# A two-layer graph network on 256 nodes: two classes' softmax weights combined ahead of the edge loop, and the mixed tiles scattered in two fp32r products

## The chip, the cores and the metric

The kernel runs on one core of a Trainium2 chip. The time is that of the device for one execution, in microseconds (us), the median of several runs; lower is better. PE is TensorE, DVE is VectorE, ACT is ScalarE, POOL is GpSimd, and SP is the engine that only starts DMAs here.

## The reference, cut to what matters

There are N = 256 nodes with D = 1024 features and E = 8192 edges sorted by destination. Each edge gets a logit, in one of three classes by its position in the list, the logits are turned into softmax weights per destination, and z is the weighted sum of the source rows. A node update and a layer norm follow, and a second attention layer behind them.

```python
feat = concatenate([n_f[edge_src], n_f[edge_dst]], axis=1)
e_hh = relu(feat[:128] @ W_hh + b_hh)
e_oo = relu(feat[128:768] @ W_oo + b_oo)
e_ho = relu(feat[768:] @ W_ho + b_ho)          # 7424 of the 8192 edges
logit = (concatenate([e_hh, e_oo, e_ho]) @ W_a + b_a)[:, 0]
ex = exp(logit - segment_max(logit)[edge_dst])
alpha = ex / segment_sum(ex)[edge_dst]
z_f = segment_sum(alpha[:, None] * n_f[edge_src], edge_dst)
nf2 = concatenate([n_f, z_f], axis=1)          # then W_hn, W_on, relu, residual, layer norm
```

## The kernel before

Edges are not handled by their weights one at a time. For each class the kernel sums logits and counts into 256 x 256 tables, `S_log` and `S_cnt`, with three kinds (0 is hh, 1 is oo, 2 is ho) and two halves h of 128 destinations each. The mean logit of a (source, destination) pair is sum by count, and the softmax over a destination's row is exp(mean - maximum) times count. P, the normalised sum of the three kinds, is transposed on PE (`PT`) and multiplied with the node features to give z (`zT`).

Weights W come by DMA in chunks of 128 rows, two a transfer, into four slots of `W_raw`, are split into a high fp32r part (`high`, on ACT, L580) and a low part (`low`, W minus high, on DVE at L906, or `lows`, on POOL at L458, for those chunks that `by_pool` names), and PE multiplies high with high, high with low and low with high. A slot is loaded again when its chunks have been used. Chunks 40 to 47 are the last half of W_ho, 48 to 79 are W_hn and W_on (`update`), 80 to 87 layer two's W. UX is 58: chunks 48 to 57 need only the node features, those from 58 on come around zT.

The hh and oo classes are small and are summed ahead of the loop. DVE forms their mean logits (`static_means`, L1078) and their row maximum in `small[:, 44:46]` (L1154 and L1155, stage "means"), while PE ends the chunks of W_ho. DVE then takes the lows of `B_tab` (L1104), for which ACT takes the highs (L657), and ACT copies the same accumulators out for the mixed rows (`target_rows`, L704). The stage "hoB_lo" behind them releases PE's second half of the first gather.

The ho class has 7424 edges, sorted by (source quarter, destination quarter) into 58 tiles of 128 edges with one pair of quarters each (NL = 58), and 4 tiles that hold what is left over from several pairs, the mixed tiles (NM = 4). For each of the 58 tiles the loop does this:

- ACT makes one-hot columns for two tiles at a time (`distance`, `onehot`, double-buffered).
- PE gathers the two table rows of each edge with them, summed in PSUM (`gather`, L1539, four fp32r products of 512 columns). There are three PSUM places, so gather t waits for the reduction of tile t - 3.
- DVE reduces each row with relu and W_a to a logit (`reduce_tile`, L1167).
- POOL makes one-hots of the keys for the scatter (`ends`), and ACT scales one of them by the logit (`scale_ends`, L692).
- PE scatters tile t - 4 into G0, the table in PSUM, logits and counts at once (`scatter`, L1554, fp32).

A mixed tile's rows are fetched by POOL's indirect DMAs, reduced on DVE ahead of the tiles in `AHEAD` (`reduce_mixed`, L1173), scaled on ACT over all four quarters (`mixed_ends`, L712), and scattered on PE `MLAG` tiles later in four fp32 products of 256 columns (`scatter_mixed`, L1548). Its one-hots `mixed_dst` and `mixed_src` are made by POOL ahead of the loop (`mixed_onehots`), in memory that later takes the highs of chunks 56 and 57 and the third kind of `S_log` and `S_cnt`.

Behind the loop PE does two chunks of the update, the last four scatters and the chunks 50 to 56. DVE copies the third kind out, forms its means and the maxima (stage "maxima"), and takes the low of chunk 56. ACT takes the exponentials of all three kinds for each half (L767), DVE multiplies and adds them (L1194 to L1196), normalises (stage "P"), takes the low of chunk 57, and copies PT (L1207). PE waits for P, transposes it, does chunk 57, and goes on to zT (L1626). In each engine the order is that of the program, with semaphores between the engines; `link` makes DVE or POOL wait for its own last instruction.

## Time and profile before

| | us |
|---|---|
| median of 3 runs | 339.38 (338.69 to 339.42) |
| the profiled execution's own time | 340.16 |
| its span, first to last instruction | 338.1 |
| PE busy | 316.6 (94%) |
| DVE busy | 281.7 (83%) |
| ACT busy | 187.4 (55%) |
| POOL busy | 121.6 (36%) |

The profile is of one execution, so durations out of it are held against its own time and not against the median. Busy shares are means over stages with different limits. Starts are in us from the first instruction. A matmul's duration contains its way through the array and overlaps with the next, so the price of one in a row of them is the distance of the starts. The granted clock of PE stands at 1.00 for 2.4 GHz and at 0.50 for 1.2 GHz.

### The profile page before, as it was taken

To read this page: it belongs to the slowest core of one execution; us is meant where nothing else is said; L and a number is where in the kernel's file an instruction comes from. 1 tells how busy PE (TensorE), PEld (TensorE's weight loads), DVE (VectorE), ACT (ScalarE), POOL (GpSimd) and SP (SyncE) were. 2 spreads that over 40 slices of the span, in tenths; PEclk is the share of its full clock that TensorE was granted. 3 is DMA by queue.
4 is the path that set the end of the run, shared out by engine and by line. 5 is a ranking of instruction groups with operands and counts; after the bars stand their busy time and mean duration, and the time that the engine had idled before them with its cause. 6 is when DMAs were issued, how large, how long until landed. Compare 5 with 4: busy or idle time off the path is not lost.

```text
span 338.1 us, 4491 instructions
## 1 busy us (share of the span) xinstructions
PE 316.6 (94%) x1438; PEld 243.4 (72%) x1438; DVE 281.7 (83%) x414; ACT 187.4 (55%) x283; POOL 121.6 (36%) x126
## 2 busy tenths in 40 slices
PE   8999999999999999889899999999799899999980
PEld 8778887776654678567788888887587686788730
DVE  0998999998979988799898998989968967883644
ACT  3765593412036336588776867657048567851355
POOL 4300042075000591819997999770000300005000
PEclk9999999999999999999999999999799999999996
DMA  7999599869999999214606303024397999000003
GB/s 220 402 404 410 193 342 381 322 239 229 281 345 305 392 416 409 106 62 75 175 2 121 123 7 126 1 64 155 101 364 245 297 339 356 8 1 0 2 1 124
DMA packets 19351, 68.86 MB, mean 204 GB/s; under 512 B 2413, under 2 KB 2413, under 8 KB 19329
## 3 DMA queue, kind: packets, MB, share of 16 engines
q1 hardware_dynamic: 13536, 50.07, 40.3%
q0 software_dynamic: 3232, 12.41, 13.4%
q10 hardware_dynamic: 2560, 6.10, 5.1%
q8 instruction: 13, 0.21, 0.3%
q14 instruction: 10, 0.07, 0.1%
HBM read 63.31 MB, written 5.26 MB: 203 GB/s over the span
## 4 chain that ended last, share of the span: by engine, by line
PE 47%; DVE 38%; ACT 5%; DMA 5%; issue 4%; POOL 0%; DVEq 0%; ACTq 0%; POOLq 0%
DVE ps L1167 10%; PE ps L1539 8%; DVE W_lo L906 7%; PE ps L1662 7%; PE ps L1371 6%; PE ps L1420 6%; PE ps L1591 5%; DMA W_raw<-in_L_gnn_W_oo_dram 5%; PE ps L1599 3%; DVE tile_val L925 2%; PE ps L1694 2%; PE ps L1626 2%; PE ps L1548 2%; PE ps L1554 1%; PE ps L1404 1%
## 5 line engine op out<-in xcount | busy, mean ns | idle before, releaser
L580 ACT CAST W_hi<-W_raw 128x1024 fp32r<-128x1024 f32 x62 | 63.0, 1047 | 51.6 <-DMA W_raw<-in_L_gnn_W_ho_dram 28.1
L1167 DVE SCALAR_TENSOR_TENSOR ps<-ps,wa_bc 128x1024 f32<-128x1024 f32 x58 | 69.2, 1253 | 5.6 <-PE ps L1539 5.6
L906 DVE TENSOR_TENSOR W_lo<-W_raw,W_hi 128x1024 fp32r<-128x1024 f32 x54 | 66.1, 1255 | 7.1 <-ACT W_hi L580 4.6
L1371 PE MATMUL ps<-W_hi,xT_hi 128*128 128x512 f32 x112 | 45.8, 409 | 0.8 <-DVE W_lo L906 0.8
L1539 PE MATMUL ps<-A_tab,oh 128*128 x116 | 41.8, 441 | 3.4 <-DVE ps L1167 3.3
L1371 PE MATMUL ps<-W_lo,xT_hi 128*128 128x512 f32 x112 | 43.7, 390 | 0.0
L1539 PE MATMUL ps<-B_tab,oh 128*128 x116 | 36.5, 396 | 0.9 <-DVEq L899 0.9
L1371 PE MATMUL ps<-W_hi,xT_lo 128*128 128x512 f32 x112 | 34.5, 389 | 0.0
L487 POOL TENSOR_SCALAR sc<-sc 128x256 f32<-128x256 f32 x29 | 28.4, 978 | 2.6
L1420 PE MATMUL ps<-W_raw,hh_x 128*128 128x512 f32 x64 | 28.2, 594 | 0.0
L686 ACT ACTIVATE oh<-oh_dist 128x512 fp32r<-128x512 bf16 x29 | 18.2, 628 | 14.6 <-PE ps L1539 14.5
L1539 PEld LDWEIGHTS ps<-B_tab,oh 128*128 128x128 f32 x116 | 21.7, 188 | 6.0 <-issue 1.3
L1371 PEld LDWEIGHTS ps<-W_hi,xT_hi 128*128 128x128 f32 x112 | 21.0, 188 | 6.8 <-issue 1.8
L485 POOL TENSOR_TENSOR sc<-irow,keys 128x256 f32<-128x256 f32 x29 | 20.9, 722 | 11.8 <-PE ps L1554 11.6
L1554 PEld LDWEIGHTS ps<-sc 128*128 128x128 f32 x116 | 21.4, 188 | 4.9
L1371 PEld LDWEIGHTS ps<-W_lo,xT_hi 128*128 128x128 f32 x112 | 21.1, 188 | 4.6 <-issue 0.7
L1371 PEld LDWEIGHTS ps<-W_hi,xT_lo 128*128 128x128 f32 x112 | 21.0, 188 | 4.5
L1539 PEld LDWEIGHTS ps<-A_tab,oh 128*128 128x128 f32 x116 | 18.3, 190 | 6.0 <-issue 5.6
L1420 PEld LDWEIGHTS ps<-W_raw,hh_x 128*128 128x128 f32 x64 | 11.9, 190 | 13.5 <-issue 13.4
L692 ACT ACTIVATE sc<-sc,keys 128x64 f32<-128x64 f32 x58 | 17.9, 339 | 6.2 <-DVE ps L1167 6.2
L679 ACT ACTIVATE oh_dist<-key_rows,pcol 128x512 bf16<-128x512 uint8 x29 | 20.5, 707 | 0.4 <-ACT mixed_row L704 0.4
L558 POOL TENSOR_SCALAR x<-x 128x2048 f32<-128x2048 f32 x1 | 5.5, 5467 | 41.5 <-DVEq L899 41.5
(328 smaller groups left out, 642.3 us busy)
## 6 DMA issues: line engine op xcount, KB each, us to landing
W_raw<-in_L_gnn_W_ho_dram SPq DMA_DIRECT2D x8, 1024.0 KB, 7.3
W_raw<-in_L_gnn_W_hh_dram SPq DMA_DIRECT2D x8, 1024.0 KB, 8.6
W_raw<-in_L_gnn_W_hn_dram SPq DMA_DIRECT2D x8, 1024.0 KB, 5.9
W_raw<-in_L_gnn_W_on_dram SPq DMA_DIRECT2D x8, 1024.0 KB, 6.8
W_raw<-in_L_gnn_W_oo_dram SPq DMA_DIRECT2D x7, 1024.0 KB, 12.1
W_raw<-in_L_gnn_W_dram SPq DMA_DIRECT2D x4, 1024.0 KB, 6.9
table_scratch<-tabs ACTq DMA_DIRECT2D x2, 1024.0 KB, 5.7
key_rows<-key_rows_scratch POOLq DMA_DIRECT2D x1, 1792.0 KB, 13.3
```

The source lines that it names most:

```text
L485: link(ga.tensor_tensor(pair, irow[:, 1:Q + 1].unsqueeze(1).unsqueeze(1).broadcast_to([P, 2, 2, Q]), keys[:, t:t + 2, 0:2].unsqueeze(3).br ...
L487: ga.tensor_scalar(pair, pair, 0.0, None, ALU.is_equal).then_inc(ends_made, 1)
L580: sa.copy(halves(n)[0], W_raw[:, n // 2 % NS, n % 2, :]).then_inc(hi_made, 1)
L679: sa.activation(oh_dist[:, j % 2, :, :], key_rows[:, :, 2 * j * P:2 * (j + 1) * P], ACT.Abs, bias=pcol[:, 1:2]).then_inc(dist_made, 1)
L686: sa.activation(oh[:, j % 2, :, :], oh_dist[:, j % 2, :, :], ACT.Relu, bias=1.0, scale=-1.0) \
L906: v.tensor_tensor(lo, W_raw[:, n // 2 % NS, n % 2, :], hi.bitcast(F32), ALU.subtract).then_inc(lo_made, 1)
L1167: v.scalar_tensor_tensor(acc, acc, 0.0, wa_bc[:], ALU.max, ALU.mult, accum_out=keys[:, t, 2:3]).then_inc(reduced, 1)
L1371: ins = mm(acc[:, m * D + f:m * D + f + 512], x_part(n - first, m), W[:, f:f + 512], start=(n == first and x_part is hi and W is W1), stop ...
L1420: ins = mm(G0[:, f:f + 512], hh_x[:, row // KC, row % KC, :], W_raw[:, n // 2 % NS, n % 2, f:f + 512], start=(row == 0), stop=(row == 2 * ...
L1539: ins = mm(acc[:, n * 512:(n + 1) * 512], oh[:, t // 2 % 2, k, t % 2 * P:(t % 2 + 1) * P], tab[:].rearrange("p q d -> p (q d)")[:, n * 512 ...
L1554: ins = mm(G0[:, bass.ds(column.with_bounds(min_val=0, max_val=15 * Q), Q)], sc[:, t % U, 1:3, :].rearrange("p r n -> p (r n)"), sc[:, t % ...
L1662: ins = mm(G1[:, m * D + f:m * D + f + 512], part[:, c, m * P:(m + 1) * P], W[:, f:f + 512], start=(c == 0 and part is xT_hi and W is W1), ...
```

## The change

It has four parts.

1. hh and oo: the exponentials of the two kinds are taken ahead of the loop, against their own maximum, multiplied by the counts and added there. Behind the loop only the third kind gets its exponential, and the combined part is rescaled by exp(own maximum - common maximum), a column of two values, inside the instruction that adds it.
2. Mixed tiles: the one-hots become fp32r, the logits are split into a high and a low fp32r part, and each mixed tile is scattered in two sets of four fp32r products, the second set (with the counts' one-hots set to zero) MLAG tiles behind the first. ACT gets a step `mixed_rest` between them.
3. AHEAD goes from (18, 24, 36, 42) to (18, 24, 33, 39), MLAG from 6 to 5.
4. The low of chunk 57 (UX - 1) goes from DVE, where it stood between P and PT, to POOL, behind its `pick` and `shift` constants. Chunk 56 stays with DVE.

`static_L`, `behind_L` and their like are second names for the memory of `S_log` and `S_cnt`.

```diff
-AHEAD = (18, 24, 36, 42)
-MLAG = 6
+AHEAD = (18, 24, 33, 39)
+MLAG = 5
...
-            return END["hoB"] <= n < UX - 2
+            return END["hoB"] <= n < UX and n != UX - 2
...
             ga.nop().then_inc(pick_made, 1)
+            lows(UX - 1, UX)
...
-                sa.activation(mixed_dst[:, r, :, 1, :], mixed_dst[:, r, :, 0, :], ACT.Copy, scale=mixed_logit[:, r:r + 1]) \
-                  .then_inc(mixed_made, 1)
+                sa.activation(mixed_dst[:, r, :, 1, :], mixed_dst[:, r, :, 0, :].bitcast(F32), ACT.Copy,
+                              scale=mixed_logit[:, r:r + 1]).then_inc(mixed_made, 1)
+                sa.copy(mixed_hi[:, r:r + 1], mixed_logit[:, r:r + 1]).then_inc(mixed_parts, 1)
+
+            def mixed_rest(r):
+
+                act.wait_ge(mixed_parts, 3 * r + 1)
+                sa.activation(mixed_lo[:, r:r + 1], mixed_hi[:, r:r + 1].bitcast(F32), ACT.Identity,
+                              bias=mixed_logit[:, r:r + 1], scale=-1.0).then_inc(mixed_parts, 1)
+                act.wait_ge(mixed_scattered, 2 * r + 1)
+                act.wait_ge(mixed_parts, 3 * r + 2)
+                sa.activation(mixed_dst[:, r, :, 1, :], mixed_dst[:, r, :, 0, :].bitcast(F32), ACT.Copy,
+                              scale=mixed_lo[:, r:r + 1]).then_inc(mixed_parts, 1)
+                act.wait_ge(mixed_parts, 3 * r + 3)
+                sa.activation(mixed_dst[:, r, :, 0, :], mixed_dst[:, r, :, 0, :].bitcast(F32), ACT.Copy,
+                              scale=0.0).then_inc(mixed_made, 1)
...
             table_high(B_tab, G1, 2, 4, 0, D // 2)
+            act.wait_ge(dve_step, dve_at("means"))
+            for h in range(2):
+                sa.activation(S_log[:, 0:2, h, :], S_log[:, 0:2, h, :], ACT.Exp, bias=small[:, 42 + h:43 + h]) \
+                    .then_inc(act_step, 1)
...
                     if (AHEAD[r] + 4) // 2 == j:
                         mixed_ends(r)
+                    if (AHEAD[r] + MLAG + 4) // 2 == j:
+                        mixed_rest(r)
...
             act.wait_ge(dve_step, dve_at("maxima"))
+            sa.activation(small[:, 42:44], small[:, 8:10], ACT.Exp).then_inc(act_step, 1)
             for h in range(2):
-                sa.activation(S_log[:, :, h, :], S_log[:, :, h, :], ACT.Exp, bias=small[:, h:h + 1]) \
+                sa.activation(S_log[:, 2, h, :], S_log[:, 2, h, :], ACT.Exp, bias=small[:, h:h + 1]) \
                     .then_inc(act_step, 1)
...
+            link(v.tensor_scalar(small[:, 42:44], small[:, 44:46], -1.0, None, ALU.mult))
             stage("means")
             low_quarter(B_tab, G1, 4, 0, 2)
             stage("hoB_lo0")
             low_quarter(B_tab, G1, 6, 2, 4, 0, D // 2)
+            dve.wait_ge(act_step, act_at("static1"))
+            link(v.tensor_tensor(S_log[:, 0:2, :, :].rearrange("p k h n -> p (k h n)"),
+                                 S_log[:, 0:2, :, :].rearrange("p k h n -> p (k h n)"),
+                                 S_cnt[:, 0:2, :, :].rearrange("p k h n -> p (k h n)"), ALU.mult))
             low_quarter(B_tab, G1, 8, 2, 4, D // 2, D // 2)
             stage("hoB_lo")
+            link(v.tensor_tensor(S_log[:, 0, :, :], S_log[:, 0, :, :], S_log[:, 1, :, :], ALU.add))
...
             link(v.tensor_scalar(small[:, 0:2], small[:, 2:4], -1.0, None, ALU.mult))
+            link(v.tensor_tensor(small[:, 8:10], small[:, 44:46], small[:, 2:4], ALU.subtract))
             stage("maxima")
             low(UX - 2)
             for h in range(2):
                 dve.wait_ge(act_step, act_at(f"soft{h}"))
-                link(v.tensor_tensor(S_log[:, :, h, :], S_log[:, :, h, :], S_cnt[:, :, h, :], ALU.mult))
-                link(v.tensor_tensor(S_log[:, 0, h, :], S_log[:, 0, h, :], S_log[:, 1, h, :], ALU.add))
-                link(v.scalar_tensor_tensor(S_log[:, 0, h, :], S_log[:, 0, h, :], 1.0, S_log[:, 2, h, :],
+                link(v.tensor_tensor(S_log[:, 2, h, :], S_log[:, 2, h, :], S_cnt[:, 2, h, :], ALU.mult))
+                link(v.scalar_tensor_tensor(S_log[:, 0, h, :], S_log[:, 0, h, :], small[:, 42 + h:43 + h], S_log[:, 2, h, :],
                                             ALU.mult, ALU.add, accum_out=small[:, 4 + h:5 + h]))
...
             stage("P")
-            low(UX - 1)
...
-                if t - MLAG in AHEAD:
-                    scatter_mixed(AHEAD.index(t - MLAG))
+                for part in range(2):
+                    if t - (1 + part) * MLAG in AHEAD:
+                        scatter_mixed(AHEAD.index(t - (1 + part) * MLAG), part)
```

## Rows read from the trace of the kernel before

**Rows 1.** The page, part 4: the chain that ended last, shares of the span.

```profile
PE 47%; DVE 38%; ACT 5%; DMA 5%; issue 4%; POOL 0%; DVEq 0%; ACTq 0%; POOLq 0%
```

**Rows 2.** The waits, 142 to 222: who waited for whom, us, times, longest.

```profile
DVE ps L1167 <- PE ps L1539: 5.6, 7, 1.6
```

**Rows 3.** Timeline of DVE in the loop: start, us, what, [idle before].

```profile
142.93 1.23 DVE L1167 SCALAR_TENSOR_TENSOR ps<-ps,wa_bc 128x1024 f32<-128x1024 f32 x1 [0.95 <-PE ps L1539]
...
186.10 1.23 DVE L1167 SCALAR_TENSOR_TENSOR ps<-ps,wa_bc 128x1024 f32<-128x1024 f32 x1 [1.57 <-PE ps L1539]
...
211.18 1.23 DVE L1167 SCALAR_TENSOR_TENSOR ps<-ps,wa_bc 128x1024 f32<-128x1024 f32 x1 [1.23 <-PE ps L1539]
...
220.60 1.26 DVE L1167 SCALAR_TENSOR_TENSOR ps<-ps,wa_bc 128x1024 f32<-128x1024 f32 x1
```

**Rows 4.** The chain in order of time, merged: start, us, what, up to the loop's end.

```profile
115.73 1.33 PE ps L1452 x12
...
208.43 1.78 PE ps L1548 x8
...
213.61 0.99 PE ps L1539 x4
214.77 0.98 PE ps L1539 x4
...
222.46 0.85 PE ps L1554 x8
```

**Rows 5.** Windows: us, busy of PE, PEld, DVE, ACT, POOL; clock, DMA share, GB/s.

```profile
200.00:210.00 10.00, 10.00 (x53) 8.57 (x51) 9.95 (x18) 6.79 (x16) 9.24 (x10) 1.00 0.30 107
...
240.00:244.00 4.00, 4.00 (x13) 3.13 (x13) 3.85 (x5) 0.00 (x0) 0.00 (x0) 0.64 0.00 0
```

**Rows 6.** Timeline of all engines ahead of the loop, 126 to 146.

```profile
134.32 0.69 DVE L1154 TENSOR_TENSOR junk<-S_log 128x512 f32<-128x512 f32 x1
...
135.88 4.04 DVE L1104 TENSOR_TENSOR B_tab<-ps,B_tab 64x1024 fp32r<-64x1024 f32 x4
...
138.45 1.01 ACT L704 COPY bias_bc<-ps 128x1024 f32<-128x1024 f32 x1 [1.00 <-DVEq L899]
...
140.56 1.42 DVE L1104 TENSOR_TENSOR B_tab<-ps,B_tab 64x512 fp32r<-64x512 f32 x2 [0.64 <-ACT B_tab L657]
...
142.17 0.72 PE L1539 MATMUL ps<-B_tab,oh 128*128 x2 [0.88 <-DVEq L899]
```

**Rows 7.** The chain in order of time behind the maxima, 230 to 300.

```profile
233.06 0.88 DVE S_log L1194
...
233.97 0.44 DVE S_log L1195
...
236.82 0.18 DVE small L1199
...
238.30 1.24 DVE lo_in_raw L906
...
239.59 2.07 PE ps L1591 x4
241.66 2.03 PE ps L1599 x6
...
268.52 0.91 PE ps L1591 x4
```

**Rows 8.** Timeline of PE, 235 to 262: the transposes of P.

```profile
238.27 0.66 PE L1615 MATMUL ps<-ident,S_log 128*128 128x128 f32 x4 [1.73 <-DVEq L899]
```

**Rows 9.** Groups by line: count, busy us, mean ns of one, idle before.

```profile
L712 ACT ACTIVATE mixed_dst<-mixed_dst,mixed_logit 128x256 f32<-128x256 f32 x4 | 2.0, 496 | 0.0
```

**Rows 10.** Timelines of DVE and POOL: a DVE reduction from SBUF, two POOL lows.

```profile
200.40 1.25 DVE L1173 SCALAR_TENSOR_TENSOR mixed_row<-mixed_row,wa_bc 128x1024 f32<-128x1024 f32 x1
...
200.99 2.93 POOL L458 TENSOR_TENSOR W_lo<-W_raw,W_hi 128x1024 fp32r<-128x1024 f32 x1
...
208.89 2.38 POOL L458 TENSOR_TENSOR lo_in_raw<-W_raw,hi 128x1024 fp32r<-128x1024 f32 x1
```

More of the change, by code:

```diff
@@ L100, in gnn_two_layers @@
         mixed_logit = sb("mixed_logit", [P, NM])
+        mixed_hi = sb("mixed_hi", [P, NM], F32R)
+        mixed_lo = sb("mixed_lo", [P, NM])
         st_logit = sb("st_logit", [P, 1 + JO])
@@ L136, in gnn_two_layers @@
         before_sums.close()
+        before_S = ExitStack()
+        static_L = sb("static_L", [P, 2, 2, N], F32, before_S)
+        behind_L = sb("behind_L", [P, 2, N], F32R, before_S)
+        static_C = sb("static_C", [P, 2, 2, N], F32, before_S)
+        behind_C = sb("behind_C", [P, N], F32R, before_S)
+        before_S.close()
         S_log = sb("S_log", [P, 3, 2, N])
@@ L191, in gnn_two_layers @@
         mixed = ExitStack()
-        mixed_dst = sb("mixed_dst", [P, NM, N // Q, 2, Q], F32, mixed)
+        mixed_dst = sb("mixed_dst", [P, NM, N // Q, 2, Q], F32R, mixed)
         mixed.close()
         hi_01 = sb("hi_01", [P, 2, D], F32R, regions)
-        behind_hi_01 = sb("behind_hi_01", [P, 2 * P], F32, regions)
+        behind_hi_01 = sb("behind_hi_01", [P, 2 * P], F32R, regions)
         key_rows = sb("key_rows", [P, 2, NL * P], U8, regions)
@@ L217, in gnn_two_layers @@
         mixed_rows = [b_ho_bc[:], bias_bc[:, 1, :], bias_bc[:, 0, :], mixed_row[:]]
-        mixed_src = [behind_hi_01[:, 0:N], S_log[:, 2, 0, :], S_log[:, 2, 1, :], S_cnt[:, 2, 0, :]]
+        mixed_src = [behind_hi_01[:, 0:N], behind_L[:, 0, :], behind_L[:, 1, :], behind_C[:]]
         tab_dram = [nc.dram_tensor(f"table{k}_scratch", [N, D], F32, kind="Internal").ap() for k in range(2)]
@@ L259, in gnn_two_layers @@
         mixed_made = sem("mixed_made")
+        mixed_parts = sem("mixed_parts")
         mixed_scattered = sem("mixed_scattered")
@@ L358, in gnn_two_layers @@
                      "x1T0a", "x1T0b", "x1T1", "h_0", "h_1", "albc", "sums", "hp0", "hp1", "hp2"]
-        ACT_STAGES = ["xT0a", "xT0b", "xT1", "hh_x", "ooB_out", "C_hh", "C_oo", "A_rows0", "A_rows1", "L_oo", "L_hh", "B_rows0", "B_rows1", "counts", "parts", "soft0", "soft1", "zT0", "both0", "zT1",
+        ACT_STAGES = ["xT0a", "xT0b", "xT1", "hh_x", "ooB_out", "C_hh", "C_oo", "A_rows0", "A_rows1", "L_oo", "L_hh", "static0", "static1", "B_rows0", "B_rows1", "counts", "parts", "rescale", "soft0", "soft1", "zT0", "both0", "zT1",
                       "both1", "q0_low", "q1_low", "sd0", "x1T0a", "sd1", "x1T0b", "x1T1", "h1_0", "h1_1a",
@@ L737, in _ @@
                     if j // 3 == 8:
-                        act.wait_ge(mixed_scattered, NM)
+                        act.wait_ge(mixed_scattered, 2 * NM)
                     high(END["hoB"] + j // 3)
@@ L1542, in gather, with scatter_mixed @@
                 ins.then_inc(gathered, 1)
-            def scatter_mixed(r):
-                pe.wait_ge(mixed_made, r + 1)
+            def scatter_mixed(r, part):
+                pe.wait_ge(mixed_made, 2 * r + part + 1)
                 for q in range(N // Q):
-                    ins = mm(G0[:, q * N:(q + 1) * N], mixed_dst[:, r, q, :, :].rearrange("p r n -> p (r n)"), mixed_src[r],
-                             start=False, stop=False, skip_group_check=True)
+                    ins = mm(G0[:, q * N:(q + 1) * N], mixed_dst[:, r, q, :, :].rearrange("p r n -> p (r n)"),
+                             mixed_src[r], start=False, stop=False, skip_group_check=True)
                 ins.then_inc(mixed_scattered, 1)
```

## The prediction

> **What bounds the kernel now.** I read the page's chain first: PE holds 47% and DVE 38% of what ended last [rows 1], so no engine bounds the whole kernel, and each edit has to be placed in its own stage. The diff touches three: the softmax statistics ahead of the 58-tile loop, the loop, and the softmax behind it.
>
> In the loop the list of waits says that DVE waited 5.6 us for PE's gathers [rows 2]. DVE back to back takes 1.18 us a tile: the starts 211.18 and 220.60 are eight tiles apart [rows 3]. With four reductions of mixed tiles at about 1.2 us its work is 58 x 1.18 + 4 x 1.2 = 73.2 us, and the loop lasted 79 us (142.93 to 220.60 + 1.26 [rows 3]). PE takes 0.99 us for a gather and 1.16 us with its scatter (the starts 213.61 and 214.77 [rows 4]), plus 1.78 us for the products of each mixed tile [rows 4]: 58 x 1.155 + 4 x 1.78 = 74.1 us (1.155 over many tiles). The two are even, so what costs is a PE burst larger than its lead. Two of the four mixed scatters made DVE idle, 1.57 us before the start at 186.10 and 1.23 before 211.18 [rows 3]; with the 0.14 us by which back-to-back reductions otherwise overlap their accumulator read that is 1.71 and 1.36 us. The rest of the 5.6 us lies in small gaps in the first 15 tiles, ahead of any mixed scatter.
>
> Behind the loop DVE is the chain: means, maxima, softmax, then the low half of the last chunk [rows 7]. PE has finished what it may do and stands idle for 1.73 us before the four transposes of P [rows 8], then 0.66 us more for that low half, and then runs its ten products in 2.07 + 2.03 us [rows 7], at a mean clock of 0.64 between 240 and 244 [rows 5]. Everything behind (zT, the rest of the update, layer two) hangs on the end of these products at 241.66 + 2.03 = 243.69: chunks, DVE lows and DMAs there are released by it or in step with it.
>
> **The change part by part.**
> *Ahead of the loop.* DVE gets one tiny operation (0.2 with its gap, as the row at 236.82 [rows 7]) before "means", and one product over 1024 columns between the B_tab lows. From 0.88 us for 768 columns [rows 7] and 0.69 for 512 [rows 6] I take 1.2 us. DVE finished its four first lows at 139.92 and began the last two at 140.56, after 0.64 us of idle time [rows 6]. Now it is at 140.1 + 1.2 = 141.3: +0.7 us (bounds 0.3, if the idle time takes more of it, and 1.4, if nothing does). ACT's two new exponentials (512 columns each, between 0.5 and 0.93 us by their neighbours; 0.65 taken) follow the B_tab copies that ended by 137.5 and end at 138.75. ACT's next item began at 138.45 [rows 6], so it slips 0.3 us, which DVE's 0.7 covers. The sum of two classes (0.69 us) comes after the last low and lies beside PE's 0.72 us of the first gather's second half [rows 6]: nothing; without that cover 0.7.
>
> *The loop.* Each mixed tile's four fp32 products (eight passes in the trace, 1.78 us, 0.22 each) become two sets of four fp32r products. No fp32r row has 256 columns. The nearest below is bf16 with 256 columns, 12 in 1.33 us, 0.111 each; above stands the full price of the fp32 product, 0.445 [rows 4], and between them fp32r with 512 columns, 0.227 (four in 0.91 us [rows 7]). Since 512 fp32r columns cost twice 0.111 and a little, I take 0.115: 0.46 us a set, eight sets 3.7 us instead of 7.1. PE's sum falls to 70.7 us, under DVE's 73.2, and a burst of 0.46 us fits under the lead that a gather has over its reduction (about a microsecond when PE is held back by its three buffers). Both gaps go, -3.07 us. Sets fall on neighbouring tiles (28 and 29, 43 and 44), where two bursts use up the lead: 0.27 given back. Net -2.8 us (0 to -3.3). The other 2.8 us of DVE's idle time stay.
> ACT pays: per mixed tile two more full activations (0.50 us, as the first [rows 9]), two on one column (0.2 each) and their waits, 1.4 us, 5.6 us in all. It was busy 6.79 of 10 us in 200 to 210 [rows 5]. mixed_rest waits for the first set on PE, and queued behind it on ACT are the next onehots, for which gathers wait. By then DVE has reduced that same tile (scale_ends stands ahead of it), so PE is past the set: no wait. At tiles 38 to 45 a high, two rests and an ends meet and the onehots run some 0.2 to 0.6 us late, under PE's lead. Nothing taken; up to 1.5. POOL writes the same one-hots; DVE's reductions of mixed tiles 2 and 3 move three tiles forward, and their rows have landed before.
>
> *Behind the last reduction.* The last scatters no longer queue behind a late update, but ACT's copy of the counts, which DVE needs next, follows the last scale and a high at an unchanged distance: -0.2 of the 0.5 us possible. Maxima gets a subtraction: +0.2. Then DVE has two rounds of 0.88 + 0.44 for product and sum and about 0.46 for the weighted sum, 3.76 us from 233.06 to 236.82; now 0.44 + 0.45 a round, 1.8 us: -1.96 (0.44 is the 256-column row [rows 7]). ACT's one-column exponential and two of 256 columns (0.3 + 0.5 until the first is ready) lie beside the low of chunk 56, 1.22 us on DVE; without it they would show.
>
> *The last chunk's low.* It leaves DVE, 1.24 us between P and the copy of PT [rows 7], and PE's wait for it, 0.66 us, goes. POOL has it (2.38 us [rows 10]) after its memsets; its earlier lows keep their place, and it should end near 225.5, eight us before use. PE's chunks 50 to 56 end at 236.5 - 2.6 = 233.9 (they follow the last scatter, which comes earlier by the loop's 2.1 and the 0.5); P is ready at 238.2 + 0.7 - 2.8 - 0.2 + 0.2 - 1.96 = 234.1. PE's idle time falls from 1.73 + 0.66 to some 0.3 us. The trace shows the clock at half only after those 2.4 us of standing, so I take it to stay at 2.4 GHz: the ten products cost 10 x 0.227 = 2.27, the price of such products elsewhere [rows 7], not 4.10: -1.83 (0 to -1.83).
>
> **Sum**, against the profiled execution (span 338.1, time 340.16): +0.7 - 2.8 - 0.2 + 0.2 - 1.96 - 0.66 - 1.83 = -6.55, so 333.6. It stands 0.78 over the median 339.38 of the three runs, which gives 332.8. What is late next is DVE through the loop, and behind it PE and DVE within 0.3 us of each other.
>
> **Rivals.**
> *A, slower: the fp32r products cost as much as the fp32 ones.* Then PE has 4 x 1.78 = 7.1 us more, less about 1.1 that it now waits for DVE, plus 0.7: the last gather is 6.7 us later. P is at 238.2 + 6.7 + 0.2 - 1.96 = 243.1, PE just done, zT starts at 243.1 + 0.7 + 2.3 = 246.2, +2.5: 341.9. It decides from about 1.47 us a set (2.5 / 8 under 1.78). Against it: the fp32r rows show one pass for each product, not two, and at 512 columns twice what bf16 costs at 256. 4%.
> *B, a product bound by its weight load, 0.227.* A set is 0.91, eight 7.3 us: DVE's gaps stay in smaller pieces. -6.55 + 2.8 = -3.75: 335.6. Against it: a scatter pass with its load takes 0.106 (eight in 0.85 us [rows 4]). 10%.
> *C, ACT comes late* in tiles 38 to 50, 1.5 us: 334.3. For it: 1.4 us per mixed tile on an engine two thirds busy. 10%.
> *D, PE's clock falls before zT all the same*: 334.7. 8%.
> *E, POOL's low in DVE's way.* At 200.99 a POOL low took 2.93 us instead of 2.38 while DVE's reduction of a mixed row from SBUF ran until 201.58 [rows 10]. If POOL is later than I think, its low starts just before DVE's two-input product behind the reciprocal, which then waits for up to 2.4 us; PE stands idle for 2.7 us and its clock falls too: 332.8 + 2.4 + 1.8 = 337.0. 7%. The Trainium skill (SBUF — State Buffer, "Who interferes with whom") says that a VectorE instruction with two SBUF inputs and a GpSimd instruction that reads SBUF exclude each other for the whole instruction, whichever issues first; by that rule E is possible in full and not only in part, and the 0.55 us that POOL lost at 200.99 agree with it.
> *F, the clock falls at the loop's start*, where PE's idle time of 0.88 us before the first gather's second half [rows 6] grows to 1.6: +1.9, 334.7. 5%.
>
> **Chances.** The forecast has 56%, by itself 331.3 to 334.3. The range 331.2 to 335.9 takes in B, C, D and F and leaves out A, E and the forecast's outer tails, two in ten. A measurement of this kernel tells 0.2% (0.7 us) from no change. Faster 0.95 (all but A and a combination), same 0.01, slower 0.04.
>
> **What would show it.** In the profile after: MATMULs of the mixed scatter in sets of about 0.46 us; the waits of DVE for PE in the loop near 2.8 us, no gap over 0.6 us behind tile 20; the first reduction 0.7 us later, the last 2.1 earlier; no chunk low on DVE between P and PT; PE's idle time ahead of the P transposes under 0.6 us, clock 1.00 there, and the ten products in 2.3 us. The prediction is wrong if sets cost over 0.7 us, if DVE waits in the loop for onehots, or if the step from P to zT stays over 4 us.

## The result, and the profile after

| | before | after |
|---|---|---|
| median of 16 executions each | 338.90 us (337.70 to 340.39) | 337.47 us (335.75 to 339.19) |
| the profiled execution's own time | 340.16 | 339.19 |
| its span | 338.1 | 337.1 |

The ratio of after to before is 0.9949, 95% interval 0.9933 to 0.9966: the change gives 1.4 us of the 6.6 that I forecast. The direction was right, the size was not, and the time lies above the range's upper end, 335.9. Both profiled executions are among the slowest of their kernel, so I read mechanisms from the two traces and sizes from medians of runs.

The page after, part 4, beside [rows 1]: PE and DVE have both lost share in the chain, 47% to 45% and 38% to 34%, and the DMAs' has grown (5% to 12%). This execution is late for the most part ahead of anything that the diff touches: its first lows of B_tab start at 137.13, before at 135.88 [rows 6], and only 0.2 us of that is part 1's small operation. POOL's fetch of mixed rows had waited 4.58 us for a DMA there, so its short instructions ran on until 134, beside DVE's `static_means`, three of which took 0.61, 0.99 and 0.51 us instead of 0.42, 0.75 and 0.43.

```profile
PE 45%; DVE 34%; DMA 12%; ACT 4%; issue 4%; SPq 0%; DVEq 0%; ACTq 0%
```

The waits of DVE in the loop, 142 to 224.5 us, against the 5.6 us of [rows 2] (waiter, releaser, us in total, times, longest):

```profile
DVE ps L1204 <- PE ps L1575: 3.5, 7, 1.2
```

They have shrunk, if not to the 2.8 that I forecast (the longest, 1.17, lies in the first tiles, where the clock is low), and the four-product sets are as cheap as forecast. This is PE's timeline with the last set but one in it (start, us; [idle before]): the tile with a set lasts 207.57 - 205.94 = 1.63 us, a tile without 1.16, so a set costs 0.47, against the 1.78 of [rows 4] for a whole scatter in one burst.

```profile
205.94 0.63 PE L1575 MATMUL ps<-A_tab,oh 128*128 x2
...
207.01 0.72 PE L1584 MATMUL ps<-behind_C,mixed_dst 128*128 128x256 f32 x4
207.57 0.63 PE L1575 MATMUL ps<-A_tab,oh 128*128 x2
```

And still the loop is not shorter. From the first reduction's start to the last one's end it took 221.86 - 142.93 = 78.93 us before [rows 3] and 224.45 - 144.91 = 79.54 after. The loss isn't idle time, which is why the list of waits doesn't have it: it sits inside a busy instruction. DVE's timeline after, at the third mixed tile (number 2), and POOL's beside it:

```profile
190.46 2.47 DVE L1210 SCALAR_TENSOR_TENSOR bias_bc<-bias_bc,wa_bc 128x1024 f32<-128x1024 f32 x1
...
189.44 2.40 POOL L467 TENSOR_TENSOR W_lo<-W_raw,W_hi 128x1024 fp32r<-128x1024 f32 x1
```

The reduction of a mixed row takes both inputs from SBUF. It took 1.25 us at 200.40 before [rows 10] and takes 2.47 here. POOL's low ends at 191.84, and 191.84 - 190.46 = 1.38 us of waiting plus 1.1 of its own give just this. The reductions of ordinary tiles, one of whose inputs is in PSUM, run beside such lows without a loss (1.26 us each beside the low at 203.76). The diff brought the two together when AHEAD moved this reduction from tile 36 to 33 while POOL_LOWS left the low behind tile 34's one-hots. The fourth mixed row (number 3) meets a short instruction of POOL, 0.62 us from 199.87, in the same way and takes 1.66 us:

```profile
199.91 1.66 DVE L1210 SCALAR_TENSOR_TENSOR mixed_row<-mixed_row,wa_bc 128x1024 f32<-128x1024 f32 x1
```

Ahead of the loop the product of the two classes stands in DVE's row between the lows of B_tab, and PE now stands for 2.98 us, where it stood for 0.88 [rows 6]; in the first tiles its clock is low (windows: us, busy of PE, PEld, DVE, ACT, POOL; clock, DMA share, GB/s):

```profile
141.20 1.22 DVE L1193 TENSOR_TENSOR S_log<-S_log,S_cnt 128x1024 f32<-128x1024 f32 x1
...
144.07 0.73 PE L1575 MATMUL ps<-B_tab,oh 128*128 x2 [2.98 <-DVEq L930]
...
142.20:150.00 7.80, 5.35 (x14) 3.41 (x14) 6.15 (x11) 4.54 (x9) 3.30 (x3) 0.78 0.25 101
```

Behind the loop it is as forecast. The two softmax rounds lasted 3.76 us by the chain [rows 7], 3.84 from the start of their first product in DVE's timeline; now the rows are 0.42 and 0.48 and both rounds end 1.97 us after 235.89, the start of theirs. PE has no idle time ahead of the transposes of P (1.73 in [rows 8]) nor behind them, and its ten products run in 0.92 + 1.40 us at full clock instead of 2.07 + 2.03 at 0.64 [rows 5, 7]. DVE's timeline, PE's chain and the window:

```profile
235.89 0.42 DVE L1232 TENSOR_TENSOR S_log<-S_log,S_cnt 128x256 f32<-128x256 f32 x1
...
239.97 0.92 PE ps L1628 x4
240.89 1.40 PE ps L1636 x6
242.29 3.45 PE ps L1663 x16
...
240.00:244.00 4.00, 4.00 (x19) 3.35 (x19) 3.84 (x4) 0.00 (x0) 0.00 (x0) 1.00 0.54 153
```

zT begins at 242.29, 1.40 us earlier than before (241.66 + 2.03 [rows 7]), where I had it 6.55 earlier.

### The profile page after: what moved, and what is told of

It reads as the page before. It is cut to its first block, busy times and chain, and to the rows that moved or that the text cites. A ratio compares the mean times of both kernels' runs of the same rounds, so it can differ in the third digit from the quotient of the medians.

```text
span 337.1 us, 4518 instructions
## 1 busy us (share of the span) xinstructions
PE 313.5 (93%) x1438; PEld 240.5 (71%) x1438; DVE 281.9 (84%) x415; ACT 192.6 (57%) x302; POOL 127.7 (38%) x127
## 4 chain that ended last, share of the span: by engine, by line
PE 45%; DVE 34%; DMA 12%; ACT 4%; issue 4%; SPq 0%; DVEq 0%; ACTq 0%
DVE ps L1204 10%; PE ps L1575 9%; DMA W_raw<-in_L_gnn_W_oo_dram 7%; PE ps L1628 7%; DVE W_lo L937 7%; PE ps L1699 7%; PE ps L1456 6%; PE ps L1636 5%; DMA W_raw<-in_L_gnn_W_ho_dram 4%; PE ps L1407 3%; DVE tile_val L956 2%; PE ps L1731 2%; PE ps L1663 2%; DVE B_tab L1135 2%; PE ps L1590 1%
## 5 line engine op out<-in xcount | busy, mean ns | idle before, releaser
L494 POOL TENSOR_TENSOR sc<-irow,keys 128x256 f32<-128x256 f32 x29 | 22.9, 790 | 11.6 <-PE ps L1590 11.4
```

The costliest lines, as they stand in the source:

```text
L494: link(ga.tensor_tensor(pair, irow[:, 1:Q + 1].unsqueeze(1).unsqueeze(1).broadcast_to([P, 2, 2, Q]), keys[:, t:t + 2, 0:2].unsqueeze(3).br ...
```

## The experiments

Four groups of runs (e1 to e3 and e7; e4, e5, e8 and e9; e10 to e13; e14 to e16), each with its own executions of the kernel before on the same chip (medians 339.28, 338.96, 338.99, 338.98); ratios are to those. "Loop" is the stretch from the first reduction's start to the last one's end in that run's trace, and "zT" the start of the first zT product.

### One part taken away, or one alone

**e1_no_static**: the changed kernel without its first part. The exponentials, the product, the sum and the rescaling ahead of the loop go, and the old softmax returns.

```diff
-            link(v.tensor_tensor(S_log[:, 0:2, :, :]..., S_cnt[:, 0:2, :, :]..., ALU.mult))
...
-                link(v.tensor_tensor(S_log[:, 2, h, :], S_log[:, 2, h, :], S_cnt[:, 2, h, :], ALU.mult))
+                link(v.tensor_tensor(S_log[:, :, h, :], S_log[:, :, h, :], S_cnt[:, :, h, :], ALU.mult))
```

> The changed kernel without its first part: all three classes' exponentials and products are again behind the loop; the fp32r sets and the moved low stay. My theory now: the product that stands on DVE between the B_tab lows (1.22 us there, 0.6 of idle time used up) makes PE stand 3.0 us ahead of the loop instead of 0.9, so that its clock falls for the first tiles; together the loop starts 1.2 to 2.0 us later and loses 0.8 more. So without it the first reduction starts near 143 again, the clock stays 1.00 in the first tiles, the last reduction ends 2 to 3 us earlier than in the changed kernel, and the softmax takes 1.96 us more, during which PE has run out of chunks and stands 1 to 2 us: about 337 us, equal to the changed kernel within 0.7. Rival (the late start is a variation of one execution and the static part costs nothing): the loop ends within 0.5 us of the changed kernel's and the time is 1.5 to 2 us longer, 339.3.

Measured: 337.93 us, ratio 0.9954 (0.9933 to 0.9976). The loop begins at 143.37 and lasts 78.60, PE stands 1.60 us ahead of P, zT at 241.49. Part 1 is worth 0.5 us in the changed kernel by the medians and 0.2 by the ratios, less than the interval can tell from nothing.

**e2_old_mixed**: the changed kernel with the fp32 scatter of before and its places.

```diff
-AHEAD = (18, 24, 33, 39)
-MLAG = 5
+AHEAD = (18, 24, 36, 42)
+MLAG = 6
...
-        mixed_dst = sb("mixed_dst", [P, NM, N // Q, 2, Q], F32R, mixed)
+        mixed_dst = sb("mixed_dst", [P, NM, N // Q, 2, Q], F32, mixed)
```

> The changed kernel without its second and third part: mixed tiles again in one set of four fp32 products, AHEAD and MLAG as before; static combination and moved low stay. My theory now: the sets gave back what they gained, because DVE's reduction of mixed tile 2 now meets a POOL low (2.40 us instead of 1.36) and DVE waits in small pieces. So the time is that of the changed kernel within 0.7: about 337.5; the mixed reductions are again all under 1.45 us, and two waits of 1.2 to 1.6 us for PE are back. Rival (my forecast of the sets was right, only the loop's start was wrong): 2.0 to 2.8 us slower than the changed kernel, 339.5 to 340.3.

Measured: 337.40, ratio 0.9946 (0.9924 to 0.9968), the same as the whole change. The loop lasts 78.85, its two waits for PE are back, and all mixed reductions are under 1.45. The fp32r scatter, to which I gave 2.8 us, is worth nothing as it stands.

**e3_only_low57**: the kernel before with the last chunk's low on POOL and nothing else of the change.

```diff
-            return END["hoB"] <= n < UX - 2
+            return END["hoB"] <= n < UX and n != UX - 2
```

> The kernel before with only the fourth part: the low of chunk 57 on POOL. PE's wait of 0.66 us for it goes; it still stands 1.7 us ahead of the transposes of P. If 1.7 us of standing is too short for the clock to fall: -0.66 - 1.83, 336.4. If the clock falls all the same: -0.66, 338.2. I hold the second likelier (60 to 40).

Measured: 338.14 (337.89 to 339.09), ratio 0.9969 (0.9950 to 0.9989). Alone it gives 1.05 us; it is the only part that was run alone. PE still stands 1.59 us ahead of P (238.13), but no longer behind the transposes, and its clock stays up.

**e7_low_back**: the changed kernel with that low back on DVE, between P and PT.

```diff
-            lows(UX - 1, UX)
...
             stage("P")
+            low(UX - 1)
```

> The changed kernel without its fourth part: the low of chunk 57 back on DVE between P and the copy of PT. Theory: PE waits about 0.5 us for it behind the transposes and the clock holds: 0.5 us slower than the changed kernel, 337.9. Rival (the clock falls): 2.3 slower, 339.7.

Measured: 338.02, ratio 0.9953 (0.9931 to 0.9975): 0.5 us above the changed kernel by the medians, 0.1 by the ratios, which isn't clear of noise. With PE no longer standing ahead of P the low costs PE 0.6 us and no clock (1.00 in 240 to 244).

### The collision

**e4_pool_lows**: the changed kernel; POOL's second low two tiles earlier.

```diff
-POOL_LOWS = (20, 34, 38, 44, 50)
+POOL_LOWS = (20, 32, 38, 44, 50)
```

> The changed kernel with one number changed: POOL takes its second chunk low behind tile 32's one-hots instead of tile 34's, about 2.4 us earlier, so that it no longer runs beside DVE's reduction of mixed tile 2. In four profiles with the new AHEAD that reduction holds DVE for 2.3 to 2.4 us, in the three with the old one for 1.36. Theory (POOL's low and a DVE instruction with two SBUF inputs exclude each other): the step falls to 1.2 to 1.4 us, the last reduction ends 1.0 us earlier, time 0.6 to 1.0 under the changed kernel's, about 336.6. Rival (the long step has another cause, such as the DMAs): the step stays at 2.3 and the time within 0.3 of 337.5.

Measured: **335.15** (334.72 to 335.90), ratio 0.9885 (0.9857 to 0.9912). One number gives 2.3 us by the medians of e9 and this run, 1.8 by their ratios, where I had expected 0.6 to 1.0. The loop lasts 77.06 and both reductions take 1.22 us. Against the loops of e5 and e11, in which the clock stays up at the start as it does here (78.67 and 78.57), that is 1.5 to 1.6 us for the two collisions. The rest has two sources outside them, and no run ties either to the changed number: the clock at the loop's start, which by the mean clocks (0.988 to 0.992) fell in none of these six executions, and a collision behind zT (see e10). In the loop, this time DVE comes first and POOL's one-hot, 0.62 us by itself, waits (DVE's timeline, then POOL's):

```profile
188.57 1.22 DVE L1210 SCALAR_TENSOR_TENSOR bias_bc<-bias_bc,wa_bc 128x1024 f32<-128x1024 f32 x1
...
188.81 1.45 POOL L494 TENSOR_TENSOR sc<-irow,keys 128x256 f32<-128x256 f32 x1
```

**e12_before_pool_lows**: the same number in the kernel before, as a control.

> The kernel before with one number changed: GpSimd's second low part two tiles earlier (POOL_LOWS 34 to 32). In it no low part of GpSimd lies beside the reduction of a mixed tile. If the 2.3 us that the same number gave in the changed kernel came from such a collision, it gives nothing here: 338.9 within 0.3, and no step of the loop shorter by more than 0.3. If instead the earlier place is better by itself, this is 1 us or more below 338.9.

Measured: 340.15, ratio 1.0032 (1.0010 to 1.0054). It isn't better by itself, as the theory had it; but it isn't neutral either, as I had expected. Moving the second low shifts when POOL is at its later ones, and the fourth one now begins 0.18 us ahead of a reduction of a mixed row, where in the kernel before it began 0.59 us behind one [rows 10]. DVE and POOL:

```profile
200.49 3.26 DVE L1173 SCALAR_TENSOR_TENSOR mixed_row<-mixed_row,wa_bc 128x1024 f32<-128x1024 f32 x1
...
200.31 2.37 POOL L458 TENSOR_TENSOR W_lo<-W_raw,W_hi 128x1024 fp32r<-128x1024 f32 x1
```

So 0.8 us in the order of two starts turn a reduction of 1.25 us into one of 3.26, and the loop from 78.93 to 80.32. That is a second instance of the mechanism, made in a kernel without the change. The clock fell ahead of zT in this trace too, but that isn't the cause: the eight executions with a mean clock of 0.990 to 0.992 have a median of 339.72, against 338.56 for the executions of the kernel before in which it stayed up (e14).

### The start of the loop

**e5_static_pool**: the changed kernel; the product and the sum of the two classes are made by POOL, behind its mixed one-hots.

```diff
...
+            pool.wait_ge(act_step, act_at("static1"))
+            link(ga.tensor_tensor(S_log[:, 0:2, :, :]..., S_cnt[:, 0:2, :, :]..., ALU.mult))
+            link(ga.tensor_tensor(S_log[:, 0, :, :], S_log[:, 0, :, :], S_log[:, 1, :, :], ALU.add))
...
```

> The changed kernel with the product and the sum of the two static classes on POOL, behind its mixed one-hots, where it waits about 7 us for the first scatters; DVE waits for it only at the softmax. Theory (the static part costs what stands on DVE ahead of the first gather's second half, 1.0 to 1.2 us, and in some executions a fall of the clock): the first reduction starts 0.9 to 1.2 us earlier, PE stands about 1.3 us there, the clock in the first tiles is 1.00, time 336.2. Rival (DVE's order there is covered by ACT's copy and nothing is gained): 337.5.

Measured: 336.51, ratio 0.9909 (0.9879 to 0.9938), 1.0 us under the changed kernel. The first reduction is at 143.42, the clock in 142 to 150 is 1.00, the reduction of the mixed row still takes 2.44.

**e11_warm**: the changed kernel with more idle products of PE ahead of the loop.

```diff
-            for _ in range(5):
+            for _ in range(14):
                 mm(bank(2), xT_hi[:, 0, 0:P], flat(xT_hi, 0, 2), start=True, stop=True, skip_group_check=True)
```

> The changed kernel with 14 instead of 5 idle products of TensorE ahead of the loop, so that it isn't idle for 3.0 us (144.07 [2.98]) before the first product of B_tab. If the low clock in the first tiles (0.79 over 142 to 150 us, a step of 2.5 instead of 1.6 at tile 1) comes from this idleness, it is gone: window at 1.00, the step at tile 1 at 1.6, and the median 0.4 to 0.85 us below the changed kernel, 336.6 to 337.1. If the low clock has another cause it stays at 0.79 and the median at 337.5.

Measured: 337.35, ratio 0.9938 (0.9915 to 0.9961). The window is at 1.00 and the step at tile 1 is 1.61, and all seven executions have a mean clock of 0.990 to 0.993, so the low clock does come from PE's standing; the median moves by 0.1 us only. But the run doesn't price the fall, because the 14 products hold PE up themselves. PE's timeline:

```profile
139.68 3.48 PE L1596 MATMUL ps<-xT_hi 128*128 128x512 f32 x14
```

They push the first B_tab product to 143.46, where it stands at 143.01 in e9 (the next run), and the first reduction to 144.20 against 143.85.

**e9_after_again**, the changed kernel once more, and **e8_before_again**, the kernel before once more:

> The changed kernel, unchanged, for a second profile. The profiled execution (339.19) was the slowest of 16. Theory: 1.2 to 1.7 us of it are particular to that execution (POOL's one-hots beside DVE's means, a first reduction at 144.9 where three other kernels with the same code start at 143.8, and the clock's fall in the first tiles). So here the first reduction starts at 143.7 to 144.0, and the same steps of DVE as in the first profile come back: 2.3 to 2.4 us at mixed tile 2, 1.4 to 1.65 at tiles 28, 29 and 31, 1.5 at 49. Time 337.4.

> The kernel before, unchanged, for the spread of its executions. Its times ahead of this lie in two heaps, about 338.5 and about 340.3. Theory: the heaps are executions in which PE's clock does not fall or falls in the 4 us ahead of zT, 1.83 us apart, so the mean clock of an execution and its time go together in two groups, and the profiled execution of before (340.16) was of the upper heap. Then my -1.83 is earned only in that heap and counts about half in a median. Rival: the times spread without any link to the clock.

Measured: 337.48, ratio 0.9937 (0.9911 to 0.9962), and 338.85, ratio 0.9995 (0.9970 to 1.0020). The traces are worth more than the medians. e9's first reduction is at 143.85 where after's is at 144.91, so 1.1 us of the late start in the trace of after belongs to that execution. PE stands for only 1.75 us in e9, and its clock falls behind that all the same. Of the 24 executions of the changed kernel (16 with the result, 8 here), 11 have a mean clock of 0.983 to 0.985 and a median of 337.73; the other 13 have 0.988 to 0.993 and 337.38. In e8's trace PE stands for 1.7 us ahead of P and 0.7 behind it as in [rows 8], and yet the clock doesn't fall:

```profile
240.00:244.00 4.00, 4.00 (x20) 3.41 (x19) 3.85 (x5) 0.00 (x0) 0.00 (x0) 1.00 0.17 34
```

Its zT begins at 241.99, 1.7 us ahead of 243.69.

### The clock ahead of zT

**e14_before_busy**: the kernel before with idle products in PE's gap ahead of P.

```diff
             update(END["hoB"] + 2, UX - 1)
+            pe.wait_ge(dve_step, dve_at("maxima"))
+            for _ in range(7):
+                mm(bank(0), xT_hi[:, 0, 0:P], flat(xT_hi, 0, 2), start=True, stop=True, skip_group_check=True)
             pe.wait_ge(dve_step, dve_at("P"))
```

> The kernel before with 7 idle products of TensorE (0.23 us each, 1.6 in all) between chunk 56 and the transposes of P, where it stands for 1.6 to 1.7 us. If the clock's fall ahead of zT costs 1.8 us in about four of ten executions of the kernel before (those of 339.5 to 341 us, with a mean clock of 0.985 to 0.988) and nothing in the others, then the upper heap is gone: all runs at 338.0 to 339.1, a mean clock of 0.989 to 0.992, and a median 0.3 to 0.6 us below that of before. If the two heaps have another cause, both stay. If my forecast's full 1.83 had been right for the median, it would be 337.1.

Measured: 338.73 (338.28 to 339.68), ratio 0.9991 (0.9975 to 1.0007). Of 100 executions of the kernel before that came with the experiments, 45 have a mean granted clock of 0.983 to 0.987 and a median of 340.14 us; the other 55 have 0.988 to 0.993 and 338.56. Of the 12 executions of e14 none is of the first kind; nor of the 12 of e3. So the fall costs 1.6 us, in not quite half of the executions. Taking it away moves the median by 0.25, which the interval doesn't tell from nothing; the median of all 100, 339.00, lies 0.44 above that of the 55. PE's timeline in e14: the gap is full, and the first of the ten products takes 0.50 instead of 0.80.

```profile
236.44 1.75 PE L1614 MATMUL ps<-xT_hi 128*128 128x512 f32 x7
...
239.65 0.50 PE L1591 MATMUL ps<-hi,x_both 128*128 128x512 f32 x1 [0.65 <-DVE lo_in_raw L906]
```

### Together, and what remains of the loop

**e10_both_pool**: e4 and e5 in one kernel.

> The changed kernel with both cures: GpSimd's second low part is issued two tiles earlier (POOL_LOWS 34 to 32), and the product and the sum of the two classes known ahead of the loop are made on GpSimd beside the loop. If the collision in the loop and the product on VectorE's path are two separate costs, they add up: alone they gave 2.3 and about 0.9 us against the changed kernel, together 3.2, so 334.2 to 334.6 us, with a first reduction at 143.3, a last one ended by 220.0 and zT0 at about 237.9. If GpSimd's product (about 5 us) collides with VectorE early in the loop, or the loop hands the gain back at fixed waits, it stays at the 335.1 of the run with the low part moved alone.

Measured: **335.03** (333.71 to 336.29), ratio 0.9872 (0.9842 to 0.9903). The first reduction comes 0.6 us earlier than in e4 (143.23), zT too (238.17 against 238.76), but the profiled time is 334.91 against e4's 334.85. The two do not add up within what six executions tell. What gives 0.6 us back in the trace lies behind zT, and looks like the same collision once more. A piece of each chain, with a row of POOL's timeline, first e10, then e4:

```profile
256.10 4.35 DVE W_lo L944 x3
258.12 2.98 POOL L572 TENSOR_SCALAR bias_bc<-bias_bc 128x1024 f32<-128x1024 f32 x1 [30.75 <-DMA bias_bc<-in_L_gnn_a_dram]
...
256.69 1.24 DVE W_lo L937
259.56 3.27 POOL L565 TENSOR_SCALAR bias_bc<-bias_bc 128x1024 f32<-128x1024 f32 x1 [31.60 <-DMA bias_bc<-in_L_gnn_a_dram]
```

POOL's sign change of bias_bc starts when its DMA has landed, and in all 17 traces one of DVE's lows beside it takes 2.06 us instead of 1.22. (DVE loses 0.84 us, not the whole length of POOL's instruction.) In e10 that is the third low of its row, and PE waits 0.8 us for it. In e4 it is the fourth, and the chain goes on from the first low without it. The fourth it is in e2 and e8 too. These three traces take 95.5 to 96.3 us from the first zT product to the end of the execution's time, the other fourteen, where it is the second or third, 96.6 to 97.1. How often each case comes in a kernel's executions no run tells.

**e13_both_pool_warm**: e10 with the 14 idle products.

> Both cures and the 14 idle products together. TensorE's clock was already 1.00 in the first tiles of the profiled runs with either cure, so if the clock falls there only in part of the executions the median moves by 0 to 0.4 us against the run with both cures: 333.9 to 334.6. If the product on VectorE was what made TensorE stand long enough, nothing is left to gain and the two are equal.

Measured: 335.72, ratio 0.9897 (0.9872 to 0.9922): no gain, as the second theory had it, and more likely a small loss. As in e11 the products last too long: the first B_tab product stands at 143.22 against 142.46 in e10, the first reduction at 143.88 against 143.23.

**e16_no_static_pool_lows**: e1 with the low at tile 32.

> The changed kernel without its first part (nothing combined ahead of the loop), with GpSimd's second low part at tile 32. In the changed kernel with the low part at 34 the first part was worth 0.5 us (337.93 against 337.47). If it stands on its own, apart from the collision in the loop, it is worth the same here: 335.15 plus 0.5 to 0.8, 335.6 to 336.0. If TensorE is what ends last behind the loop when the loop is short, the softmax's saving is lost and this run is at 335.1 or below, since the product on VectorE's path ahead of the loop is gone.

Measured: 336.28, ratio 0.9910 (0.9882 to 0.9937), 1.1 us above e4. The loop begins 1.1 us earlier than e4's and ends at 219.76 against 220.91, but P comes later and PE stands for 1.59 us ahead of it; zT at 239.28 against 238.76. So part 1 gives 0.5 us at zT here, and PE's end isn't what limits it; the rest of the difference between these two traces lies behind zT and goes with POOL's sign change, which meets the third low here and the fourth in e4. The two intervals overlap.

**e15_sets_apart**: e4 with the second mixed tile's reduction one tile later, so that its sets stand at 30 and 35.

```diff
-AHEAD = (18, 24, 33, 39)
+AHEAD = (18, 25, 33, 39)
```

> The run with the low part moved alone (335.15), and besides the second mixed tile's reduction at tile 25 instead of 24, so that its two sets of products stand at 30 and 35 and none at 29, next to that of tile 28. If the steps of 1.4 and 1.63 at tiles 28 and 29 come from two sets side by side, they shrink to 1.2 to 1.3 and the loop from 77.06 to about 76.5: 334.5 to 334.8 us. If TensorE's stall of 0.41 at that place of the program makes them, they stay, and the time stays at 335.1 within 0.3.

Measured: 336.05, ratio 0.9907 (0.9878 to 0.9936). The steps at tiles 28 and 29 are 1.18 us instead of 1.40 and 1.63 (the first of them is 1.37 in the kernel before too, where no set stands beside it). But the reduction of mixed row 1, just ahead of them, now meets one of POOL's short instructions, and that of row 3 again, 1.66 and 1.68 us instead of 1.22. The first of these delays DVE by 0.4 us, a lead for PE that would by itself hide most of the 0.67 us of the two waits; so this run doesn't tell whether neighbouring sets make them, and that stays open. In its trace the clock falls at the loop's start besides (0.79 in 142 to 150). The collisions explain only part of the missed time. In the loop, 1.0 us longer than e4's, they cost 0.8 and the clock 0.8, less the 0.67 of the two steps; and the three executions with the clock at 0.986 take 336.50 to 336.87, the three at 0.988 and 0.989 only 335.39 to 335.60. DVE's timeline:

```profile
177.67 1.66 DVE L1210 SCALAR_TENSOR_TENSOR bias_bc<-bias_bc,wa_bc 128x1024 f32<-128x1024 f32 x1
```

## Why the prediction was wrong in size, and where it was right

*The loop, forecast -2.8 (0 to -3.3), measured -0.3.* This is the step that failed: the moved reductions of mixed rows 2 and 3 were taken at their old length of about 1.2 us, with nothing for what POOL does beside them, and they took 2.47 and 1.66. The loop lasts 78.91 us in e3, where it is that of before, and 78.60 in e1, which has the new scatter and the old start. The inputs on PE's side of the term were right: sets of 0.47 us (0.46 forecast), DVE's two old gaps gone (the steps of 2.89 and 2.54 us are now 1.18 or nearly), and rival B's 0.91 a set is refuted. What I passed over stands in my own text as half a sentence, that "DVE's reductions of mixed tiles 2 and 3 move three tiles forward, and their rows have landed before". I asked whether the data would be there, not what POOL would be doing at that moment.

Of the 3.07 us of the two gaps, the collisions took back 1.2 us at mixed row 2 and 0.4 at row 3; the rest went into waits at tile 29 (0.45, where I had given back 0.27), at 31 (0.4), and at 44 and 49 (0.15 and 0.35, the latter behind a single set, which I had under PE's lead). The wait at 31 isn't rival C. The onehot behind ACT's mixed_rest is the one for tile 34 and was not waited for, and in e15, where mixed_rest comes one pair of tiles later, the step is still 1.56; PE stands for 0.25 us ahead of its gather for tile 32, and the profile names a reduction as what ended it; but the one that this gather waits for, tile 29's, had ended at 186.2, and the gather starts at 188.09. Why stays open.

With the collisions gone, parts 2 and 3 are worth 337.40 - 335.15 = 2.25 us (2.1 by the ratios of e2 and e4), of which the loop has 78.85 - 77.06 = 1.79. So even then the loop is 1.0 short of the forecast, by these waits. None of my three signs of being wrong came: a set cost 0.47, no reduction waited for a onehot, and P to zT took 3.1 us. They looked at waits and at PE, and the loss sat in DVE's busy time.

*The mechanism was among my rivals, in the wrong place.* Rival E was POOL's low in DVE's way, at 7%, priced at the reciprocal behind the loop, because I looked only where the diff adds a low to POOL. Yet the row that I drew it from [rows 10] is in the loop, at the reduction of mixed row 3. Where I had priced it, it cost next to nothing: DVE's product behind the reciprocal took 0.79 us instead of 0.69. The Trainium skill (SBUF — State Buffer, "Who interferes with whom") says that a VectorE instruction with two SBUF inputs and a GpSimd instruction that reads SBUF exclude each other, and that the order of issue decides who waits. The traces of the loop agree in both directions: DVE's 1.22 becomes 2.47 or 3.26 when POOL is first, POOL's 0.62 becomes 1.45 when DVE is. Behind zT (e10) a low of DVE loses only 0.84 us beside an instruction of POOL listed with about 3.

*The clock, forecast -1.83, worth 0.25 (e14) to 0.44 in the median.* This is the second step that failed, by its size. The mechanism was right and e3, e14 and the trace of after show it. But I took its whole price from one profiled execution in which the clock fell, and 55 of 100 executions of the same kernel don't have the fall. The 0.78 us by which that execution lay above the median was a sign of this; I subtracted it at the end and left the term whole. The Trainium skill (TensorE: Matmul & The Clock Gate, "What's actually happening") says that the point at which the clock rises under work varies from run to run. That is of a rise; for a fall that comes in some executions only, the 45 and the 55 are what shows it here.

*The start of the loop, forecast +0.70 (0.3 to 1.4), measured +1.1.* First reduction 142.72 in e3 and 143.79 in e2: the product took 1.22 us as taken, and hardly any idle time of DVE absorbed it. In the seven traces without part 1 the first reduction is at 142.69 to 143.37, in the seven with its product on DVE at 143.74 to 144.91. Rival F, the clock falling at the loop's start, did happen in the profiled executions of after, e7, e9 and e15, in each of which the step at tile 1 is 2.2 to 2.5 us instead of 1.6. I priced it at 1.9, for which I showed no sum. It costs 0.8 in the steps of e9's first four tiles, and in the changed kernel's medians 337.73 stands against 337.38 (e9 above). So the change took away one fall, ahead of zT, and brought in another, at the loop's start, in 11 of 24 executions.

*The softmax, forecast -1.96, measured 3.84 - 1.97 = 1.87*, right. *The subtraction, +0.20*: 0.16 and its gap, right. *The tail, -0.20*: nothing (1.47 us from the last reduction to the copy before, 1.49 after). *PE's wait for the low, -0.66*: gone, right.

With the measured terms the sum is +1.1 - 0.3 + 0.2 - 1.9 - 0.66 - 0.25 = -1.8 us, and the medians differ by 1.43. The loop's miss alone, 2.5 us on 332.8, would have ended at 335.3, and the clock's alone, 1.6, at 334.4, both inside the range; together they pass its end. *Rival A*, the slower side, is refuted by the 0.47 us of a set. *Rival D* didn't occur: the clock ahead of zT is 1.00 in all traces of the changed kernel.

**The better version.** e4 changes one number of the changed kernel and takes 335.15 us, 1.15% under the kernel before; e10 at 335.03 is as fast within the intervals. Both beat both kernels. With six executions each, none of e4's with the fall at the loop's start, their lead may be some tenths smaller.

## What to carry to other kernels

When an instruction of DVE with both inputs in SBUF is moved in time, ask what POOL runs at its new place, as one asks whether its data are there: in e12 the order of two starts 0.2 us apart cost 2 us, and in all these traces the loss shows as a longer busy instruction, never as a wait. The same goes for an instruction of POOL that a DMA releases: where it falls differs from one execution to the next, and with it who pays. Look in the groups by form for one line whose instructions differ in duration, before trusting a list of waits. And a price read at a reduced clock belongs to that execution; weigh it by how many executions share the reduced mean clock before it enters a sum for the median.

## What the runs showed of the hardware that I had not expected

- DVE's reduction of a 128x1024 row from SBUF takes 1.22 us, 1.62 to 1.68 beside one of POOL's short instructions, 2.36 to 2.47 behind a low of POOL, and 3.26 in e12, where POOL's low had begun 0.18 us earlier.
- fp32r products with 256 columns cost 0.47 us a set of four, 0.117 each, where an fp32 product cost 0.445.
- PE stood for 1.7 us and, 0.66 us of transposes later, 0.66 again, in both traces of the kernel before, and its clock fell in one of them; so it did in e12, which stands in the same way. In the 100 executions, 45 have the lower mean clock.
- One of DVE's lows behind zT takes 2.06 us instead of 1.22 in all 17 traces, beside POOL's sign change of bias_bc, and the time goes with which one it is: 95.5 to 96.3 us from zT to the end where it is the fourth, 96.6 to 97.1 where it is the second or third.
- Moving one low of POOL by two tiles changed the time by -2.3 us in one kernel and by +1.1 in the other.
